# Six terms in DRAM, the second layer's keys in the fill of the first attention, and a new order of masks and maxima

## The reference

```
layer 0: x += cross_attention(LN(x), ctx, key mask);  x += self_attention(LN(x));  x += moe(LN(x))
layer 1: x = LN(x + causal self_attention(x));  x = LN(x + cross_attention(x, ctx));  x = LN(x + ffn(x));  x = moe(x)
scores = q k^T / sqrt(8);  masked keys get the lowest float;  softmax;  times v;  times Wproj
```

## Time and profile before

| | us |
|---|---|
| median of 3 runs (2729.42 to 2733.01) | 2730.98 |
| profiled execution | 2728.58 |
| its span | 2726.7 |
| busy: PE / DVE / ACT / POOL | 2384.8 / 2352.2 / 2134.0 / 274.8 |

### The profile page before, as it was taken

One profiled execution on the slowest core, in us unless ns is written; L12 is line 12 of the kernel. 1 busy time (PEld: TensorE's weight loads), 2 busy tenths in 40 slices (PEclk: granted clock), 3 DMA queues, 4 the chain that ended last, 5 costly groups with the idle time before them and its releaser, 6 DMA issues.

```text
span 2726.7 us, 59202 instructions
## 1 busy us (share of the span) xinstructions
PE 2384.8 (87%) x23163; PEld 751.8 (28%) x23163; DVE 2352.2 (86%) x2668; ACT 2134.0 (78%) x4065; POOL 274.8 (10%) x740
## 2 busy tenths in 40 slices
PE   4499999999999999489758848999999999999986
PEld 2222222222222222122322213222222222222224
DVE  6699999999999997499636649999999999999945
ACT  3189999999889899469615625999999999999971
POOL 5000110012111110100001100000000100000000
PEclk8799999999999999789878968999999999999998
DMA  4201111111111110111121030111111111111000
GB/s 144 73 24 41 41 35 45 43 44 41 47 49 41 41 43 7 46 50 33 36 61 41 30 99 4 38 34 30 30 40 33 30 30 41 31 30 32 17 3 8
DMA packets 75513, 107.98 MB, mean 40 GB/s; under 512 B 17061, under 2 KB 55849, under 8 KB 75241
## 3 DMA queue, kind: packets, MB, share of 16 engines
q1 hardware_dynamic: 73128, 99.79, 12.4%
q0 software_dynamic: 2112, 4.42, 0.9%
HBM read 73.45 MB, written 21.90 MB: 35 GB/s over the span
## 4 chain that ended last, share of the span: by engine, by line
PE 68%; DVE 18%; ACT 5%; SPq 3%; issue 3%; DMA 2%; POOL 0%; ACTq 0%; DVEq 0%
PE ps L1498 68%; DVE maxima L1234 12%; ACT probs L1028 4%; SPq L515 1%; DVE maxima L1193 1%; SPq L600 1%; ACT probs L986 1%; DVE scratch L1104 1%; DMA o_self<-acc_out 0%; PE ps L1504 0%; DVE stats L1110 0%; DMA scratch<-o_self 0%; DMA q_stages<-max_rows 0%; DVE z L1104 0%; DMA q_stages<-q_cross 0%
## 5 line engine op out<-in xcount | busy, mean ns | idle before, releaser
L1234 DVE TENSOR_REDUCE maxima<-ps 128x1 f32<-128x920 f32 x1792 | 1887.8, 1111 | 96.4 <-PE ps L1498 96.3
L1028 ACT ACTIVATE probs<-ps 128x512 f32<-128x512 f32 (+1 forms) x3264 | 1761.3, 594 | 159.9 <-PE ps L1498 159.7
L1498 PE MATMUL ps<-probs,v_stage 128*16 128x256 f32 x14208 | 1159.5, 393 | 0.6 <-ACT acc_out L1017 0.4
L1498 PE MATMUL ps<-k_stages,q_stages 64*128 64x460 bf16 (+2 forms) x4032 | 756.3, 373 | 187.3 <-DMA q_stages<-q_cross 64.4
L1498 PE MATMUL ps<-q_stages,k_stages 64*128 64x512 bf16 (+1 forms) x3712 | 725.8, 381 | 45.1 <-ACT probs L986 16.9
L1498 PEld LDWEIGHTS ps<-k_stages,q_stages 64*128 64x128 bf16 x4032 | 193.6, 93 | 1049.7 <-issue 494.3
L1498 PEld LDWEIGHTS ps<-probs,v_stage 128*16 128x16 f32 x14208 | 236.9, 94 | 412.2 <-issue 362.9
L1193 DVE TENSOR_REDUCE maxima<-ps 128x2 f32<-128x1024 f32 (+1 forms) x224 | 240.1, 1108 | 94.5 <-PE ps L1498 90.9
L986 ACT ACTIVATE probs<-ps 128x512 f32<-128x512 f32 x448 | 224.2, 554 | 72.7 <-PE ps L1498 71.7
L1498 PEld LDWEIGHTS ps<-q_stages,k_stages 64*128 64x128 bf16 x3712 | 187.4, 93 | 277.4 <-ACT probs L1028 69.4
L952 ACT ACTIVATE by_key<-ps 128x512 f32<-128x512 f32 (+1 forms) x30 | 17.5, 583 | 146.2 <-PE ps L1498 146.2
(11 more groups left out here) (233 smaller groups left out, 965.4 us busy)
## 6 DMA issues: line engine op xcount, KB each, us to landing
q_stages<-q_cross SPq DMA_DIRECT2D x256, 48.0 KB, 2.6
k_stages<-k_cross SPq DMA_DIRECT2D x64, 150.2 KB
k_stages<-k_cross SPq DMA_DIRECT2D x64, 150.0 KB
scratch<-acc_out SPq DMA_DIRECT2D x496, 16.0 KB
k_stages<-k_cross SPq DMA_DIRECT2D x64, 100.1 KB
k_stages<-k_cross SPq DMA_DIRECT2D x64, 100.0 KB
q_stages<-q_self SPq DMA_DIRECT2D x32, 192.0 KB
k_cross<-probs SPq DMA_DIRECT2D x12, 384.0 KB, 2.8
```

What stands on the lines that cost most here:

```text
L1028: return nc.scalar.activation(probs[0:m, probs_slot(a, j, i), :], ps[0:m, b_bank(a, use), :], ACT.Exp, scale=float(E) ** -0.5)
L1234: nc.vector.tensor_reduce(maxima[:, at, seg:seg + 1], ps[:, A_BANK + 2 * (k % 2):A_BANK + 2 * (k % 2) + 2, 0:a.segment], AX_XY, ALU.max).t ...
L1498: return nc.tensor.matmul(out_, lhsT, rhs, start=start, stop=stop)
```

## The change

1. Setup: the mask is no longer multiplied in, only its row is written. It is loaded to one partition, x is loaded behind the first part of the context and turned between key jobs (`SETUP_TURNS`), POOL's constants come after its work for pass 0, and the mask rows and rows of ones take 4 DMAs.
2. DRAM holds six terms: three DMAs store a job, of 3, 2 and 1 terms, for keys as for queries. Staging takes one DMA of 48 rows per side. The last job of each attention is stored by ACT's queue. In the self attentions only part of pair 0's queries is staged before PE starts (`stage_rest` brings the others).
3. The 13 early key jobs leave the passes and stand in the ahead phase of cross0 (`a.fill`), with bank 6 of their own; ACT copies and rounds, POOL takes rest and part 3, SP stores. ACT waits for all their stores before its first exp.
4. self1: where the turn of the maxima is in step 0, SP puts the next maxima before it stages; on PE a step's last unit A and its B come before both masks.

The core of the diff:

```
-    early = {(a.early_from + 2 + i) * n + 4: i for i in range(early_jobs)}
-    a.items, a.items_with = [], [0]
...
+    n, banks = len(a.max_units), ceil_div(a.key_tiles, 4)
+    a.fill = [("values", i, n * (i + 1) // banks - (n * (i + 1) % banks == 0)) for i in range(banks)]
+    a.fill += [("key", i, 2 * i + 1) for i in range(early_jobs)]
+    a.fill = [[(kind, i) for kind, i, at in a.fill if at == g] for g in range(n)]
...
-        keep = probs_b[:, 0:S // 2].bitcast(BF16)
-        mask_in = probs_b[:, S // 2:S // 2 + S // 4].bitcast(U8)
-        drop_row = k_stages[0:1, 0:S]
+        drop_row = probs_b[0:1, 0:S // 2].bitcast(BF16)
+        mask_in = probs_b[0:1, S // 2:S // 2 + S // 4].bitcast(U8)
...
-            a.k_dram = dram("k_" + a.name, [3, P, a.keys], BF16)
-            a.q_dram = dram("q_" + a.name, [H, TERMS * E, N], BF16)
-            a.staged_before = sum(b.stagings // b.ring * b.stage_dmas for b in before)
+            a.k_dram = dram("k_" + a.name, [TERMS, P, a.keys], BF16)
+            a.q_dram = dram("q_" + a.name, [TERMS, P, N], BF16)
...
+        def store_job(queue, a, i):
+            kind, c0, n = a.jobs[i]
+            src, done = a.parts[:, i % SPLITS, :, 0:n], stored(a, i)
+            queue.wait_ge(sem("split_part3"), a.jobs_before + i + 1)
+            first = 0
+            for part, terms in enumerate((3, 2, 1)):
+                if kind == "k":
+                    dst, part_ = a.k_dram, src[:, 0:terms]
+                else:
+                    dst, part_ = a.q_dram, src[:, part:part + 1].to_broadcast([P, terms, n])
+                queue.dma_start(dst[first:first + terms, :, c0:c0 + n].rearrange("a p c -> p a c"),
+                                part_).then_inc(done, DMA)
+                first += terms
...
-                    for slot in range(cross0.ring):
-                        sp.dma_start(k_stages[row:row + 1, slot * WIDTH:slot * WIDTH + count],
-                                     drop_row[:, first:first + count]).then_inc(sem("rows_in"), DMA)
-                        for q in (qa_stage, qb_stage):
-                            sp.dma_start(q[row:row + 1, slot, :], ones_row[:]).then_inc(sem("rows_in"), DMA)
...
+                    sp.dma_start(k_stages[row:row + 1].rearrange("p (s w) -> p s w", s=cross0.ring)[:, :, 0:count],
+                                 drop_row[:, first:first + count].unsqueeze(1).to_broadcast([1, cross0.ring, count])
+                                 ).then_inc(sem("rows_in"), DMA)
...
-                    for row, parts_ in ((0, 3), (3 * E, 2), (5 * E, 1)):
-                        sp.dma_start(dst[base + row:base + row + parts_ * E, 0:count],
-                                     a.k_dram[0:parts_, h * E:(h + 1) * E, first:first + count]).then_inc(done, DMA)
+                    sp.dma_start(dst[base:base + ROW_MAX, 0:count],
+                                 a.k_dram[:, h * E:(h + 1) * E, first:first + count]).then_inc(done, DMA)
...
-                put_maxima(0)
+                if a is cross0:
+                    for i in range(len(early.jobs)):
+                        if i == len(early.jobs) - 2:
+                            put_maxima(0)
+                        store_job(sp, early, i)
+                else:
+                    put_maxima(0)
...
-                        for row, parts_ in ((0, 3), (3 * E, 2), (5 * E, 1)):
-                            sp.dma_start(k_stage(a, slot)[base + row:base + row + parts_ * E, :],
-                                         a.k_dram[0:parts_, h * E:(h + 1) * E, :]).then_inc(done, DMA)
-                        sp.dma_start(q_stages[base:base + ROW_MAX, :, slot, :],
-                                     a.q_dram[h].unsqueeze(1).to_broadcast([ROW_MAX, 2, N])).then_inc(done, DMA)
+                        sp.dma_start(k_stage(a, slot)[base:base + ROW_MAX, :],
+                                     a.k_dram[:, h * E:(h + 1) * E, :]).then_inc(done, DMA)
+                        if pair == 0:
+                            sp.dma_start(qa_stage[base:base + ROW_MAX, slot, 0:BANK],
+                                         a.q_dram[:, h * E:(h + 1) * E, 0:BANK]).then_inc(done, DMA)
+                            continue
...
                 for j in range(a.n):
                     pair, half = a.passes[j]
+                    if a.turn_step[j] == 0 and j + 1 < a.n:
+                        put_maxima(j + 1)
                     if half == 0 and pair >= 1 and pair + a.ring - 1 < H // 2:
                         sp.wait_ge(sem(a.name + "_scores"),
                                    pair_tile_use(a, j - 1, len(a.steps[j - 1]) - 1, a.sides - 1) + 1)
                         stage(pair + a.ring - 1)
-                    if j + 1 < a.n:
+                    if a.turn_step[j] != 0 and j + 1 < a.n:
                         put_maxima(j + 1)
...
+                for i, (_, _, n) in enumerate(early.jobs):
+                    b = i % SPLITS
+                    pool.wait_ge(sem("split_part1"), early.jobs_before + i + 1)
+                    if i >= SPLITS:
+                        pool.wait_ge(sem("split_part3"), early.jobs_before + i - SPLITS + 1)
+                    nc.gpsimd.tensor_tensor(early.rest[:, b, 0:n], early.whole[:, b, 0:n], early.parts[:, b, 0, 0:n],
+                                            ALU.subtract).then_inc(sem("split_rest"), 1)
+                    if i >= 1:
+                        take_part3(i - 1)
...
+                if a is cross0:
+                    split_early()
...
+            def take_early(i):
+                _, _, n = early.jobs[i]
+                b = i % SPLITS
+                act.wait_ge(sem("split_psum"), early.jobs_before + i + 1)
+                if i >= SPLITS:
+                    act.wait_ge(sem("split_rest"), early.jobs_before + i - SPLITS + 1)
+                    act.wait_ge(stored(early, i - SPLITS), stored_count(early, i - SPLITS))
+                whole = early.whole[:, b, 0:n]
+                nc.scalar.activation(whole, ps[:, EARLY_BANK, 0:n], ACT.Copy).then_inc(sem("early_whole"), 1)
+                act.wait_ge(sem("early_whole"), i + 1)
+                nc.scalar.activation(early.parts[:, b, 0, 0:n], whole, ACT.Copy).then_inc(sem("split_part1"), 1)
+                if i >= 1:
+                    early_part2(i - 1)
...
+                def mask_a(g):
+                    j, u = a.all_units[g]
+                    qt, c, n = a.units[j][u]
+                    if a.causal and c + n == (qt + 1) * P:
                         for side in range(a.sides):
-                            last = mm(ps[:, bank + side, n - P:n], ident_b[:], causal_a[:], start=False)
-                    last.then_inc(sem(a.name + "_max_scores"), 1)
+                            last = mm(ps[:, A_BANK + 2 * (g % 2) + side, n - P:n], ident_b[:], causal_a[:], start=False)
+                        last.then_inc(sem(a.name + "_max_scores"), 1)
...
-                    for g in range(given, goal):
+                    for g in range(given, goal - 1):
                         pass_a(g)
+                        mask_a(g)
+                    if goal > given:
+                        pass_a(goal - 1)
+                    pass_b(j, t)
+                    if goal > given:
+                        mask_a(goal - 1)
+                    mask_b(j, t)
                     given = goal
-                    pass_b(j, t)
...
+                def project_early(i):
+                    _, c0, keys = early.jobs[i]
+                    if i == 0:
+                        pe.wait_ge(sem("early_weight_in"), DMA)
+                    else:
+                        pe.wait_ge(sem("early_whole"), i)
+                    mm(ps[:, EARLY_BANK, 0:keys], flat(W["k_cross1"]),
+                       ctxT[:, c0:c0 + keys]).then_inc(sem("split_psum"), 1)
...
+                    for kind, i in a.fill[g] if g < n else []:
+                        if kind == "values":
                             project_values(a, i, kT, w_v)
+                        else:
+                            project_early(i)
```

410 lines of the change are left out of this document (210 added, 200 removed).

## The result

The changed kernel takes 2700.56 us, the median of 4 runs (2695.64 to 2704.93), against 2731.74 us before (4 runs). The ratio is 0.9886, with a 95% interval from 0.9867 to 0.9905: 31 us faster. 2664 us was forecast, with a range from 2640 to 2699. The profiled execution took 2699.43 us, its span is 2697.7 us.

The account below looks back on a forecast made before the run. PE, with 68% of the chain of waits, and stretches where PE stands empty were taken to bound the kernel. Terms -33.5 + 15.5 - 13.6 - 10 - 12.5 - 13 = -67 took 2731 to 2664 us, range 2640 to 2699.

Parts of the forecast that it names:

- Setup: Start to first maximum unit: first unit at 60 us, 33.5 us earlier (15 to 38).
- Ahead phase: First maximum unit to cross0's first scores: 13 early key jobs added, 15.5 us longer (+8 to +30).
- Early keys: cross0's passes: the 13 early keys leave them, 13.6 us off in full.
- self0 and self1 start: Starts of both self attentions: fewer query issues and fewer staging DMAs awaited, 5 us less each (3 to 8), -10.
- cross1: Start of cross1: queries' stores split three each between SP and ACT, -12.5 us (-5 to -16).
- self1: Steady part of self1: maxima put first (-7 us) and masks together (-6 us), together -13 us.
- so they go: -7: self1: with maxima put before staging, about seven waits for the maxima's DMAs vanish, -7 us (to -9).
- The sign that I named for self1: self1: no wait for the maxima's rows, listed among what would show the forecast right.
- Rival 1: self1's order brings nothing, since DVE and ACT set its steps and freed PE time becomes waiting; 2677 us, chance 0.20.
- case 3: Setup and ahead phase: DMA at only 203 GB/s, 3.9 us a job; whole 2697 us, chance 0.13.
- Masks: self1: keeping masks together saves 94 changes of form on PE, 6 us taken (0 to 9.9).

Follow-up runs that it names:

- e7: e3 with each key job of cross0 also storing its three parts once more, to a DRAM tensor nothing reads; 2693.02 us, ratio 0.986.
- e10: e9 with cross0's keys alone stored in three terms by one DMA and staged by three per side; 2668.25 us, ratio 0.9772.
- e5: e3 with only pass 0 of cross0 staged before the early keys' stores, passes 1 to 3 behind jobs 3, 7 and 12; 2683.89 us, ratio 0.983.
- e6: e3 with all keys stored in three terms by one DMA and staged by three DMAs per side, queries still six terms; 2705.48 us, ratio 0.9912.
- e9: e3 with the 13 early key jobs put back into passes 18 to 30, stored in six terms by SP; 2675.51 us, ratio 0.9799.
- e1: Changed kernel with SP's old order in self1 (stage, put maxima, store results), masks still together; 2686.90 us, ratio 0.9842.
- e2: Changed kernel with each mask product of self1 right behind its own scores again, SP's new order kept; 2712.37 us, ratio 0.9927.
- e4: Changed kernel with the edits of e1 and e2 together, both old orders in self1; 2691.79 us, ratio 0.985.
- e3: Changed kernel, but where self1's maxima go first SP stores the results right behind them and stages last; 2675.77 us, ratio 0.9795.
- e11: e3 with each mask product of self1 right behind its own scores again; 2681.20 us, ratio 0.9822.

## Why the prediction was wrong, step by step

**Setup: right, 5 us too much.** The pace of jobs (2.36 us) and its cause (all DMA engines busy) were right, and e7 shows the cause. That the key stores ended at 49.6 us as summed is partly luck: they began 1.3 us late and each was 0.1 us quicker. Behind them the queries landed 2.9 us late, and staging pass 0 was mis-sized by 2 us: 7.9 us from that landing, 6 taken. The transfer of the key rows did fall, from 9.6 to 6.3 us, but not as far as 203 GB/s would have brought it; and I left out that it queues behind the stores of both query jobs, which fill every engine until about 57 us. An estimate by the Trainium skill, "DMA: Bandwidth & Descriptors", section "Why a DMA increments its semaphore by 16 and not by 1", was that six engines with eight rows a side take 8/17, or 0.47, of the time before. The records show 6.3/9.6, or 0.66, so the direction agrees and the size does not. In e10, with three-term staging and its ten issues, it takes 59.7 - 44.8 = 14.9 us from the first issue, against 11.1 with six terms.

**Ahead phase: right.** To the first scores it is 56.7 us where the sum said 57.7; against 42.5 before that sum is +15.2, not the +15.5 written. A pair of units with both fills takes 2.45 to 2.75 us, 2.9 said. The stop of ACT was there with 5.9 us (4 said), and by e5 it does come from the four stagings ahead of the first early store. Only the way was another: SP was free in time, and it was the landing behind them that was late, 8.9 us. In e6 SP itself was late too, until 79.6 us, and the stop grew to 18.9.

**Early keys: right.** -12.4 for -13.6, and 13.3 by e9. The two terms cancel, which the prediction's sum already said (-13.6 + 15.5); e9 shows it.

**self0 and self1 start: half.** -5.4 for -10 together with self0's own passes. To the first unit it is -3.2 at self0 and -2.9 at self1, at the low end of the 3 to 8 taken. SP has fewer stores to issue there, but they land later, after 4.2 us in the median and up to 5.6 (2.4 and up to 3.1 before), so that at self0 the first staging stands 10.7 us behind the first store and not 11.6. At self1 PE then waits 1.8 us for the first maxima's rows, which stand behind the stagings, as in e6.

**cross1: right in size, wrong in cause.** -13.7 for -12.5, but by e6 fewer issues of queries bring nothing without staging the keys by 8 DMAs rather than 24. The cost of those 24 was not in their 19.92 us of issue, which lay beside other work, but in what was queued behind them in the DMA engines. That the number was met is luck.

**self1: the step that failed is "so they go: -7".** The waits for the maxima's rows did go. The step followed the DMAs that were moved forward and not the one that was thereby moved back. The results' store had stood right behind the maxima, and I looked at the waits that were there, in which it did not occur. By e1, and by e2 against e4, this edit costs 15.9 to 17.3 us of the stretch rather than giving 7; the clock lost at each stop is part of it. With the store kept right behind the maxima it gives 11.3 us (e3 against e1) and 13.7 (e11 against e4), more than the 7 taken, since each wait that goes also gives back clock.

The rows of before could have shown it. There the next copy comes at 1507.51, 2.5 us after the store's last issue. The new order puts the 4.5 us of staging between the maxima, whose rows ACT has copied at 1498.9, and the store: 1.5 + 4.5 + 2.5 us later it would have been issued, at 1507.4, when the next copy already wants it landed. With the 2.5 us that it had to land before, that is an estimate of 2.4 us of wait for each pair staged; up to 5.9 were measured. Had the row been read as a queue of three customers, with the time at which each is wanted, it would have been a rival; none of mine had it. The sign that I named for self1, no wait for the maxima's rows, came true while the stretch grew.

Rival 1, the nearest, put the worst of self1 at zero. The end of the range, 2699, came from case 3, slow stores at 2697. The measured 2700.56 lies beside it by chance: the stores took 2.36 us each and not 3.9.

**Masks: right.** 6.4, 7.7 and 4.0 us of the stretch in three pairs at different clocks, 6 said (0 to 9.9).

With -13 in place of +14.8 the kernel would stand at 2673 us; e3 does with 2675.8.

## What to carry to other kernels

When a DMA is moved forward in an in-order queue, list every DMA that it passes and every one that is now behind something longer, and for each the instruction that waits for its landing; an item that shows no wait before can be the next to decide. The maxima behind the stagings of four pairs, in e6, are the same case at the start of an attention. Two edits that take work from one phase to another should be priced as a pair and tried as a pair. Widening stores to make loads simpler pays where the DMA engines are idle (cross1's start, 14 us) and costs where they set the pace (cross0's setup, 8 us), so the layout is chosen per tensor.
